# Building self-attention's fused weights from 32-column matmuls in four column groups, each matrix as its load lands, and issuing later stages' weights in other periods

## The reference, cut to what matters

```python
q_lat = (x @ Wq_down).reshape(b, t, H, L)      # 16 heads, latent size 64
k_lat = (x @ Wk_down).reshape(b, t, H, L)
v_lat = (x @ Wv_down).reshape(b, t, H, L)
q_c = jnp.einsum('bthl,ld->bhtd', q_lat, Wq_up_c)   # and q_e, k_c, k_e
v = jnp.einsum('bthl,ld->bhtd', v_lat, Wv_up)
q = jnp.concatenate([q_c, _apply_rope(q_e, cos, sin)], axis=-1)
...
att = jax.nn.softmax(scores, axis=-1)
return y @ Wc
...
x = _layernorm(x + _L0_attn_ref(x, ...), axis=-1)
```

## Time and profile before

| | |
|---|---|
| median of three runs | 2525.32 us (2520.55 to 2530.87) |
| profiled execution | 2539.31 us |
| its span | 2537.5 us |
| its mean granted TensorE clock | 0.887 |
| self-attention's share | about the first 397 us |

### The profile page before, as it was taken

The page is one execution under the profiler, slowest core; times in us unless marked ns, Lnnn a source line. Parts: engine busy times, 40 slices in busy tenths (PEclk is TensorE's granted clock), DMA queues, the critical chain, the costliest instruction groups (busy, mean ns, idle before and its releaser), DMA issues. The chain is left out here.

```text
span 2537.5 us, 58466 instructions
## 1 busy us (share of the span) xinstructions
PE 2118.6 (83%) x20310; PEld 1583.7 (62%) x20310; DVE 1530.8 (60%) x3550; ACT 950.6 (37%) x1881; POOL 928.1 (37%) x913
## 2 busy tenths in 40 slices
PE   6999997999776664788489996999999999996575
PEld 4666665777676554566388884666666666664233
DVE  1444443555454546233255455799999999984898
ACT  1444442333210110233134342344444444442897
POOL 0111111111134555223355431455555555553343
PEclk9999998999887786899789897899999999997555
DMA  6000003555311110877233311011110101000111
GB/s 208 30 29 29 29 25 130 207 205 212 133 48 35 34 33 23 259 222 221 73 100 90 98 44 46 21 32 31 32 32 23 32 31 32 30 13 9 52 58 46
DMA packets 157643, 192.74 MB, mean 76 GB/s; under 512 B 28517, under 2 KB 141160, under 8 KB 157559
## 3 DMA queue, kind: packets, MB, share of 16 engines
q1 hardware_dynamic: 147287, 189.03, 23.7%
q0 software_dynamic: 10272, 2.62, 0.5%
HBM read 140.74 MB, written 77.51 MB: 86 GB/s over the span
## 5 line engine op out<-in xcount | busy, mean ns | idle before, releaser
L2757 ACT ACTIVATE xa_prob<-xa_A 121x1600 f32<-121x1600 f32 x96 | 144.5, 1505 | 304.1 <-PE xa_A L2636 304.1
L2828 POOL TENSOR_TENSOR xa_prob<-xa_prob,xa_exp_bias 121x1600 f32<-121x1600 f32 x64 | 228.7, 3573 | 41.0 <-ACT xa_prob L2757 40.9
L2929 DVE TENSOR_REDUCE xa_kq<-xa_A 100x4 f32<-100x1444 f32 x128 | 211.6, 1653 | 21.3 <-PE xa_A L2609 21.1
L1409 POOL DMA_INDIRECT slot_rows<-rt_x_again,rt_slot_u x150 | 152.6, 1017 | 166.0 <-DVE rt_x_again L1527 103.5
L2909 DVE TENSOR_SCALAR xa_rows_n<-xa_rows_t,xa_mv,xa_rstd 121x256 f32<-121x256 f32 x128 | 142.4, 1172 | 1.1 <-POOL xa_rstd L2845 1.1
L2636 PEld LDWEIGHTS xa_A<-xa_q2T,xa_kqT 17*121 17x121 f32 x3072 | 93.9, 185 | 56.5 <-DVE xa_kq L2929 35.9
L696 DVE TENSOR_REDUCE sa_kq<-sa_A 100x16 f32<-100x1600 f32 x32 | 58.4, 1826 | 106.1 <-PE sa_A L457 106.1
L2609 PE MATMUL xa_A<-xa_kqT 16*100 16x361 f32 x1024 | 112.9, 510 | 9.9 <-ACT xa_prob L2757 6.8
L2636 PE MATMUL xa_A<-xa_q2T,xa_kqT 17*121 17x100 f32 x3072 | 109.3, 280 | 13.8 <-DVE xa_kq L2929 13.2
L1655 POOL DMA_INDIRECT contrib<-ex_y,ex_place_u x64 | 62.3, 973 | 158.5 <-ACT ex_y L1707 140.4
L2850 POOL TENSOR_TENSOR xa_o_rstd<-xa_o_var,xa_power 100x1 f32<-100x1 f32 x32 | 17.9, 560 | 252.1 <-DVE xa_o_var L2969 252.1
(11 more groups left out here) (350 smaller groups left out, 5397.0 us busy)
## 6 DMA issues: line engine op xcount, KB each, us to landing
ex_w<-in_w13T SPq DMA_DIRECT2D x64, 352.0 KB
contrib<-xs_zero SPq DMA_DIRECT2D x30, 640.0 KB
la_rows<-contrib SPq DMA_DIRECT2D x16, 1200.0 KB
xs_ctxT<-in_ctxT SPq DMA_DIRECT2D x32, 512.0 KB
xa_rows_t<-in_ctx SPq DMA_DIRECT2D x96, 121.0 KB
ex_w<-in_w2T SPq DMA_DIRECT2D x64, 176.0 KB
slot_rows<-xs_zero SPq DMA_DIRECT2D x32, 272.0 KB
ex_x_t<-slot_rows SPq DMA_DIRECT2D x64, 136.0 KB, 2.2
```

Source lines behind the costliest of these rows:

```text
L1409: nc.gpsimd.indirect_dma_start(slot_rows, bass.IndirectOffsetOnAxis(slot_u[:, k, n:n + 1], 0), x_again[:, k, :], None, bounds_check=SLOTS ...
L2757: nc.scalar.activation(prob[:, n, :].rearrange("p (h a) -> p h a", h=HPG), A[:ROWS, :, 0:G * T], ACT.Exp, scale=EXP_SCALE).then_inc(exp_re ...
L2828: nc.gpsimd.tensor_tensor(chunk, chunk, exp_bias[:, n, :].unsqueeze(1).to_broadcast([ROWS, HEADS, T]), ALU.mult).then_inc(biased, 1)
L2929: nc.vector.tensor_reduce(kq[:T, k, NCH, 4 * j:4 * j + 4, DH:DH + 1].rearrange("p h o -> p (h o)"), A[:T, :, 0:src_len], axis=AXIS_X, op=A ...
```

## The change

`up` is put together on the host as one array `L0_attn_up` (128x3x2x16, zeros included) and loaded by one DMA; its memset and the waits for it go. The loads have semaphores of their own (`up_in` for up and ident, `down_in[k]` for each `down`), SyncE's order is up, down 0, ident, the first rows, down 1, down 2, wc, cos, sin, causalf, and it no longer waits for them.

TensorE's matmuls change sides: the 32 columns of `up` are stationary, 256 columns of `down` move, and the result (32x256, the fused weights turned on their side) goes to one of four groups of 32 PSUM partitions: 24 matmuls instead of 48. ScalarE copies each matrix (128x512) to `turned_w`; TensorE turns it back with four 128x128 transposes into `C[k]`; VectorE copies it to `wqk` or `wv`. TensorE's order is fuse(0), fuse(1), turn(0), fuse(2), turn(1), turn(2). VectorE's casts of ident and causalf stand behind its three copies; ScalarE waits for all three copies before its loop.

SyncE issues the later stages' weights in periods -1 to 3, now behind `residual` and ahead of `store`: strided in -1, cross in 0, ffn in 1, route and lists in 2, linear in 3.

```diff
--- before.py
+++ after.py
@@ -281,6 +281,7 @@
         s = Store(nc, ctx, "sa", 2)
         down = s.sb("down", [P, 3, HEADS // 2, D])
         up = s.sb("up", [P, 3, 2, DH])
+        turned_w = s.sb("turned_w", [P, 3, 2 * D])
         wqk = s.sb("wqk", [P, KC, 2 * D])
         wv = s.sb("wv", [P, KC, D])
         wc = s.sb("wc", [P, KC, D])
@@ -316,8 +317,9 @@
         C = [s.ps(f"C{k}", [P, 512]) for k in range(4)]
 
         w_in = s.sem("weights_loaded")
-        up_zero, up_ready, cleared = s.sem("up_zero"), s.sem("up_ready"), s.sem("cleared")
+        up_in, down_in, cleared = s.sem("up_in"), [s.sem(f"down_in{k}") for k in range(3)], s.sem("cleared")
         fused, fused_sb = s.sem("fused_in_psum"), s.sem("fused_in_sbuf")
+        fused_turned, turned_w_ready = s.sem("fused_turned"), s.sem("turned_w_ready")
         const_ready, power_set = s.sem("const_ready"), s.sem("power_set")
         x_loaded = [s.sem(f"x_loaded{k}") for k in range(2)]
         res_loaded = [s.sem(f"res_loaded{k}") for k in range(2)]
@@ -334,7 +336,7 @@
         yT_turned, yT_ready, o_done, r_ready = (s.sem(n) for n in ("yT_turned", "yT_ready", "o_done", "r_ready"))
         o_stats_ready, o_mv_ready, o_var_ready, o_rstd_ready = (s.sem(n) for n in ("o_stats_ready", "o_mv_ready", "o_var_ready", "o_rstd_ready"))
         out_ready = s.sem("out_ready")
-        W_ALL = 16 * 18
+        W_ALL = 16 * 4
         FIRST, LAST, REACH, LOW = -3, 3, 4, 4
 
         with nc.Block() as block:
@@ -359,30 +361,25 @@
                     sp.wait_ge(out_ready, at(b, 1, 1))
                     sp.dma_start(x_out[b[0] * 2 + b[1]], x_o[:, k, :]).then_inc(stored[k], 16)
 
+                sp.dma_start(up[:], w["L0_attn_up"]).then_inc(up_in, 16)
                 for k, name in enumerate(("L0_attn_Wq_down", "L0_attn_Wk_down", "L0_attn_Wv_down")):
-                    sp.dma_start(down[:, k, :, :], w[name].rearrange("(h l) c -> l h c", l=P)).then_inc(w_in, 16)
-                sp.wait_ge(up_zero, 1)
-                for head, part in ((0, slice(0, 64)), (1, slice(64, 128))):
-                    for k, (c_, e_) in enumerate((("Wq_up_c", "Wq_up_e"), ("Wk_up_c", "Wk_up_e"))):
-                        sp.dma_start(up[part, k, head, 0:E2], w["L0_attn_" + c_]).then_inc(w_in, 16)
-                        sp.dma_start(up[part, k, head, E2:DH], w["L0_attn_" + e_]).then_inc(w_in, 16)
-                    sp.dma_start(up[part, 2, head, :], w["L0_attn_Wv_up"]).then_inc(w_in, 16)
-                sp.dma_start(ident[:], w["ident"]).then_inc(w_in, 16)
+                    sp.dma_start(down[:, k, :, :], w[name].rearrange("(h l) c -> l h c", l=P)).then_inc(down_in[k], 16)
+                    if k == 0:
+                        sp.dma_start(ident[:], w["ident"]).then_inc(up_in, 16)
+                        rows((0, 0))
                 sp.dma_start(wc[:], w["L0_attn_Wc"].rearrange("(k p) n -> p k n", p=P)).then_inc(w_in, 16)
                 sp.dma_start(cos[:], w["cos_sa_rows"]).then_inc(w_in, 16)
                 sp.dma_start(sin[:], w["sin_sa_rows"]).then_inc(w_in, 16)
                 sp.dma_start(causalf[:], w["causal"]).then_inc(w_in, 16)
-                rows((0, 0))
-                sp.wait_ge(w_in, W_ALL)
 
                 def body(b, has):
                     if has(4):
                         rows(later(b, 4))
-                    if b[1] < 0:
-                        for held in later_weights[b[1] - FIRST::-FIRST]:
-                            held.load(sp)
                     if has(-1):
                         residual(later(b, -1))
+                    if -1 <= b[1] < LOW:
+                        for held in later_weights[b[1] + 1]:
+                            held.load(sp)
                     if has(-3):
                         store(later(b, -3))
 
@@ -395,15 +392,32 @@
                 for sem, per in ((x_turned, 1), (qk_done, 1), (kq_turned, 2), (scored, 1), (q2_turned, 1), (shifted, 1), (v_done, 1),
                                  (av_done, 1), (y_turned, 1), (yT_turned, 1), (o_done, 1)):
                     pe.sem_inc(sem, per * LEAD)
+                pe.wait_ge(up_in, 32)
+
+                def fuse(k):
+                    pe.wait_ge(down_in[k], 16)
+                    for h in range(HEADS // 2):
+                        m, g = divmod(h, 4)
+                        last = nc.tensor.matmul(A[32 * g:32 * g + 32, k, m * D:(m + 1) * D], up[:, k, :, :].rearrange("p two d -> p (two d)"),
+                                                down[:, k, h, :], start=True, stop=True)
+                    last.then_inc(fused, 1)
+
+                def turn_fused(k):
+                    pe.wait_ge(turned_w_ready, k + 1)
+                    for c in range(KC):
+                        for m in range(KC):
+                            o = c * D + m * P
+                            last = nc.tensor.transpose(C[k][:, o:o + P], turned_w[:, k, m * D + c * P:m * D + (c + 1) * P], ident[:])
+                    last.then_inc(fused_turned, 1)
+
+                fuse(0)
+                fuse(1)
+                turn_fused(0)
+                fuse(2)
+                turn_fused(1)
+                turn_fused(2)
                 pe.wait_ge(w_in, W_ALL)
-                pe.wait_ge(up_zero, 1)
-                for k in range(3):
-                    for c in range(KC):
-                        for h in range(HEADS // 2):
-                            last = nc.tensor.matmul(A[:, k, c * D + 2 * h * DH:c * D + 2 * (h + 1) * DH], down[:, k, h, c * P:(c + 1) * P],
-                                                    up[:, k, :, :], start=True, stop=True)
-                last.then_inc(fused, 1)
-                pe.wait_ge(fused_sb, 1)
+                pe.wait_ge(fused_sb, 3)
                 pe.wait_ge(const_ready, 1)
 
                 def turn_rows(b):
@@ -557,11 +571,11 @@
                 for sem, per in ((xT_ready, 1), (copied, 1), (kqT_ready, 2), (q2_ready, 1), (exp_ready, 1), (v_ready, 1), (oT_ready, 1),
                                  (yT_ready, 1)):
                     act.sem_inc(sem, per * LEAD)
-                act.wait_ge(fused, 1)
-                for k, dst in ((0, wqk[:, :, D:2 * D]), (1, wqk[:, :, 0:D]), (2, wv[:])):
-                    last = nc.scalar.activation(dst, A[:, k, :].rearrange("p (c n) -> p c n", n=D), ACT.Copy)
-                last.then_inc(fused_sb, 1)
+                for k in range(3):
+                    act.wait_ge(fused, k + 1)
+                    nc.scalar.activation(turned_w[:, k, :], A[:, k, :], ACT.Copy).then_inc(turned_w_ready, 1)
                 act.wait_ge(cleared, 2)
+                act.wait_ge(fused_sb, 3)
 
                 def queries_out(b):
                     act.wait_ge(q2_turned, at(b, 1, 1))
@@ -669,7 +683,6 @@
 
             @block.vector
             def _(dve):
-                nc.vector.memset(up[:], 0.0).then_inc(up_zero, 1)
                 nc.vector.memset(v1[:], 1.0)
                 nc.vector.memset(kq[:], 0.0).then_inc(cleared, 1)
                 dve.wait_ge(cleared, 1)
@@ -677,6 +690,15 @@
                 for sem, per in ((roped, 1), (max_ready, 1), (rec_ready, 1), (y_ready, 1), (r_ready, 1), (o_stats_ready, 1), (o_mv_ready, 1),
                                  (o_var_ready, 1), (out_ready, 1)):
                     dve.sem_inc(sem, per * LEAD)
+
+                def fused_out(k, dst):
+                    dve.wait_ge(fused_turned, k + 1)
+                    nc.vector.tensor_copy(dst, C[k][:].rearrange("p (c n) -> p c n", n=D)).then_inc(fused_sb, 1)
+
+                fused_out(0, wqk[:, :, D:2 * D])
+                fused_out(1, wqk[:, :, 0:D])
+                fused_out(2, wv[:])
+                dve.wait_ge(up_in, 32)
                 dve.wait_ge(w_in, W_ALL)
                 nc.vector.tensor_copy(identb[:], ident[:T, :T])
                 nc.vector.tensor_copy(causal[:], causalf[:]).then_inc(const_ready, 1)
@@ -3455,7 +3477,7 @@
     lists_w = ExpertLists(nc, w)
     route_w = RouteWeights(nc, w)
     strided_w = StridedWeights(nc, w)
-    self_attention(nc, NB, x, x1, w, (strided_w, route_w, lists_w, linear_w, cross_w, ffn_w))
+    self_attention(nc, NB, x, x1, w, ((strided_w,), (cross_w,), (ffn_w,), (route_w, lists_w), (linear_w,)))
     cross_attention_strided(nc, NB, x1, x2, w, src_len, slot_rows, contrib, strided_w)
     route(nc, NB, x2, w, slot_rows, xz, route_w, ffn_w)
     experts(nc, NB, w, slot_rows, contrib, lists_w)
@@ -3531,8 +3553,12 @@
     o = {}
     for k in ("Wq_down", "Wk_down", "Wv_down"):
         o["L0_attn_" + k] = x["L0_attn_" + k].T
-    for k in ("Wq_up_c", "Wq_up_e", "Wk_up_c", "Wk_up_e", "Wv_up", "Wc"):
-        o["L0_attn_" + k] = x["L0_attn_" + k]
+    ups = [np.concatenate([x["L0_attn_" + n] for n in names], 1) for names in (("Wq_up_c", "Wq_up_e"), ("Wk_up_c", "Wk_up_e"), ("Wv_up",))]
+    o["L0_attn_up"] = np.zeros((P, 3, 2, DH), ups[0].dtype)
+    for k, up in enumerate(ups):
+        for head in range(2):
```

(2 more changed lines are left out.)

## The result

In the first comparison the changed kernel takes 2517.64 us, the median of eight runs (2505.72 to 2526.04); before takes 2531.51 us over its eight (2520.55 to 2539.12). The ratio is 0.9944, with a 95% interval of 0.9916 to 0.9971: faster by 14 us, between 7 and 21. The forecast was 2504 us, within 2492 to 2515, from a saving of 21 us. The direction held, and so did the saving in the place where it was forecast; the time lies 2.6 us above the range. Two later comparisons of the same kernel gave 0.9894 (0.9866 to 0.9922) and 0.9904 (0.9868 to 0.9940), 27 and 24 us. Three executions with a mean granted clock of 0.34 to 0.73 (3076.70 us of before; 2756.41 and 6005.97 us of the old fused part with the new periods) enter no ratio.

The account below looks back on a forecast made before the run. The serial prologue before the loop was taken as exposed: its chain 12.7 + 2.2 + 1.0 + 1.0 + 0.7 + 0.34 + 0.2 = 18.1 us instead of 39.27 saves 21.2, so 2525.3 - 21.2 = 2504.1 us, range 2492 to 2515.

Parts of the forecast that it names:

- third `down` there: Prologue loads: last byte of the third `down` at 12.5 us, 0.2 to its semaphore, so 12.7, at most 14.5.
- hops: Prologue chain: 0.2 us in all for handing over between engines.
- all terms are for the slow clock: Prologue: TensorE taken at half rate, 1.2 GHz, for every term of the chain, until about 66 us in before.
- rival 1: Loop start: clock already up before the loop, so its 11 us slow start goes too: 2493 us; chance 0.13.
- the long fused stretch ahead of the loop changes nothing about the clock: Prologue: 20.7 us of busy matmuls hadn't raised the clock, so the loop's start was expected slow for about the same stretch.
- a rise one period earlier or later: Loop start: the clock rising a period sooner or later moves the end by some 5 us, most of the range.
- Column groups that don't overlap: Prologue matmuls: groups run one after another, 7.5 us a matrix instead of 2.2, giving 2519 us; chance 0.09.
- Bundles in the way: Self-attention periods: later-weight bundles in SyncE's queue delay `rows` or stores; 2531 us if all 26.6 us are exposed; chance 0.03.
- Saved time given back: Loop start: a slow stretch two periods (10 us) longer, or SyncE stalling on the third `down`: 2514 us; chance 0.1.
- the base of the sum: Whole kernel: the median of before, 2525.3 us, from which the 21.2 us saving was subtracted.
- theory B: Stages behind self-attention: the change makes them give back some 8 us; 2146 to 2150 us there, 10 to 16 faster overall.
- theory A: Stages behind self-attention: they spread from run to run whatever stands ahead; the prologue's 21 us are all kept.

Follow-up runs that it names:

- old fused part with the new periods: Kernel before, fused part unchanged, with the later weights issued in the new periods -1 to 3: ratio to before 1.0006 (0.9972 to 1.0040).
- filler: Changed kernel plus matmuls with unused results where TensorE waits, in the prologue and periods -3 to -1: 2497.74 us over 6 runs, ratio to before 0.9883.
- old matmuls: Changed kernel's loads and waits for each matrix, with the old matmuls (32 moving columns, no turn): 2526.45 us in one run, before 2510.68.
- eight in one group: Changed kernel with eight more matmuls behind matrix 0's, all in column group 0: 2369.23 us in one run, before 2387.10.
- after, second: The changed kernel again, no edit: 2505.42 us over 12 runs, ratio to before 0.9894 (0.9866 to 0.9922).
- after, third: The changed kernel a third time, no edit, beside the second filler run: ratio to before 0.9904 (0.9868 to 0.9940).
- old periods: Changed kernel with the later weights issued in periods -3 to -1, ahead of the residuals, as before: 2502.20 us over 6 runs, ratio to before 0.9892.
- filler, second: The kernel with filler matmuls in prologue and periods -3 to -1 again, beside the changed kernel: ratio to before 0.9874 (0.9846 to 0.9902).
- pairs: Changed kernel with a matrix's matmuls in order 0, 4, 1, 5, 2, 6, 3, 7, so neighbours share a column group: 2502.38 us in one run, before 2510.68.
- all in: Changed kernel, but TensorE waits for all weights before fuse(0): 2519.80 us in one run, before 2510.68.
- late filler: Changed kernel with filler matmuls only behind turn_fused(2) and in periods -3 to -1: 2379.89 us in one run, before 2387.10.

## Why the prediction was right or wrong

**The chain, term by term.**

| term | forecast | measured |
|---|---|---|
| third `down` there | 12.7 (at most 14.5) | 13.85 |
| fuse(2) | 2.2 | 1.75 |
| turn(1), turn(2) | 2.0 | 1.45 |
| VectorE copy of 512 columns | 0.7 | 0.69 |
| casts | 0.34 | 0.32 |
| hops | 0.2 | 0.26 |
| first `turn_rows` | 18.1 | 18.2 |

The end is right to 0.1 us by luck, for two errors cancel. The load came 1.2 us later than I took, inside the bound. In its first 13.8 us the profile has 263 GB/s, 3.6 MB, which is 0.3 MB more than the loads up to the third `down` hold. Either bytes of the loads behind it were moved among its own, or its semaphore came some 0.8 us behind its last byte; the traces don't tell which. The matmuls were faster, because my "all terms are for the slow clock" was wrong behind 15 us: eight turns took 1.45 us where four had taken 1.12. That is the beginning of rival 1. (Fuse, turn, fuse, turn changes the mode three times, not four as I wrote; no term hangs on it.)

**The clock in the loop's start.** The granted clock of the changed kernel (stretch, us, busy time of each engine, granted clock, DMA) shows a middle course between my forecast and rival 1:

```profile
17.00:18.00 1.00, 0.00 (x0) 0.00 (x0) 0.93 (x3) 0.00 (x0) 0.00 (x0) 1.00 0.00 0
18.00:19.00 1.00, 0.36 (x2) 0.20 (x2) 0.00 (x0) 0.23 (x1) 0.00 (x0) 0.85 0.00 0
19.00:20.00 1.00, 0.84 (x1) 0.41 (x2) 0.00 (x0) 0.11 (x1) 0.00 (x0) 0.50 0.21 63
22.00:23.00 1.00, 0.57 (x2) 0.00 (x0) 0.39 (x2) 0.00 (x0) 0.00 (x0) 0.94 0.00 0
25.00:26.00 1.00, 0.56 (x7) 0.36 (x5) 0.00 (x0) 0.75 (x2) 0.00 (x0) 0.76 0.53 159
26.00:27.00 1.00, 0.80 (x3) 0.55 (x4) 0.00 (x0) 0.15 (x1) 0.00 (x0) 0.50 0.88 303
32.00:33.00 1.00, 0.76 (x2) 0.00 (x0) 0.20 (x1) 0.00 (x0) 0.00 (x0) 0.82 0.07 23
33.00:34.00 1.00, 0.00 (x0) 0.00 (x0) 0.56 (x2) 0.38 (x1) 0.37 (x1) 1.00 0.00 0
```

It falls at 18.7, around the first `turn_rows`, is back from 22.1 to 25.5, falls again and is up from 32.4 on; so it had risen before 18.7. In before, by the durations, it came up near 66 us, 27 us into the loop. The fills with filler, 36.8 and 36.9 us, are what the same steps take at full rate. By them the slow clock in the fill costs 46.5 - 36.8 = 9.7 us in before (forecast 11) and 4.4 in the changed kernel. That accounts for the 25 us in self-attention in this pair of profiles: 21.1 from the chain and 5.3 from an earlier rise, of which 1 to 2 are lost in its other periods. I had said that the long fused stretch ahead of the loop changes nothing about the clock. That held for the old matmuls, also in the new loads (`keys_and_queries` still takes 3.73 us at 41.29 there), and not for the new ones.

The 5.3 us are one pair. The other profile with the old fused part has a fill of 42.7 us and `keys_and_queries` at 1.96 us a period earlier than before has it; against it the changed kernel's fill is only 1.5 us shorter. This part of the forecast, a rise one period earlier or later that moves the end by some 5 us, came true. By the start of `cross_attention_strided` (404.3 and 406.7 us with the old fused part, 380.6 to 382.7 in the five profiles with the new one, neither filler nor a longer wait) the change saves 22 to 26 us. At the end the three comparisons give 14, 27 and 24 us. Weighted by their intervals they come to 21 us, give or take 4, so whether the gain at the end is 21 or 25 isn't shown.

The Trainium skill, TensorE: Matmul & The Clock Gate, "What's actually happening", has the clock follow recent activity; the traces agree: matmuls in the gaps kept it at full rate through the fill in three of three profiles, and without them it fell again in all seven profiles in which it had risen ahead of the loop. The Trainium skill, TensorEngine Tiling, "Key Properties", has a change of mode drain TensorE; the traces show no cost of it: turn(0) ends at 13.83 and fuse(2) starts at 13.85, in the moment in which its load is there too.

**Rivals.** The clock up before the loop: in part, as told. Column groups that don't overlap: refuted by the eight in one group. Bundles in the way: no wait, and two comparisons with nothing. Saved time given back: 9 us were missing at the end of the first trace, but not by the mechanism that I named, and not because of the change.

**The step that failed: the base of the sum, and the spread of the untouched stages, which I put at nothing.** I wrote that the profiled execution of before stood 14 us above the median and that no term depends on why, took the median of three runs as the base, and named the clock in the loop's start, some 5 us, as most of my range. Eleven profiles, on chips on which these stages took alike, show what that left out. Behind self-attention the stages took, from `cross_attention_strided`'s start to the end of the span:

| kernel | us | `linear_attention` | its granted clock | `cross_attention` |
|---|---|---|---|---|
| before | 2130.8 | 296.4 | 0.89 | 794.8 |
| after | 2139.7 | 300.0 | 0.88 | 794.8 |
| after, second | 2139.7 | 300.7 | 0.87 | 794.1 |
| after, third | 2129.4 | 287.6 | 0.91 | 790.2 |
| old periods | 2121.4 | 293.9 | 0.89 | 790.4 |
| old fused part, new periods | 2125.9 | 290.0 | 0.91 | 794.8 |
| filler | 2113.0 | 286.3 | 0.92 | 790.4 |
| filler, second | 2140.0 | 299.1 | 0.88 | 794.4 |
| pairs | 2119.2 | 289.8 | 0.91 | 794.6 |
| all in | 2133.1 | 302.1 | 0.87 | 794.7 |
| old matmuls | 2128.4 | 299.0 | 0.88 | 789.8 |

The sum ranges over 27 us, and one kernel covers it alone: 2113.0 and 2140.0 with filler. The changed kernel has 2129.4 beside 2139.7, so theory B's mark of 2148 (counted from self-attention's last instruction) isn't its own: its third profile has 2137.9 there. The nine profiles with the new loads average 2129.3 us, the two with the old ones 2128.4. Most of the spread is TensorE's clock. Two kernels' rows for `linear_attention`, first the filler's, then that with all weights awaited (columns: stretch, us, busy of PE, PEld, DVE, ACT, POOL, granted clock, DMA share, GB/s):

```profile
1230.00:1516.30 286.30, 257.09 (x1821) 230.11 (x1821) 151.61 (x454) 114.47 (x269) 139.13 (x122) 0.92 0.29 82
```

```profile
1236.70:1538.80 302.10, 273.35 (x1820) 244.76 (x1821) 150.67 (x454) 115.00 (x269) 137.91 (x122) 0.87 0.27 77
```

`linear_attention` works through the same instructions in 286.3 us at 0.92 and in 302.1 at 0.87. The busy time of TensorE's matmuls grows by 16.3 us with it, and that of VectorE, ScalarE and GpSimd stays within 1.3 us. The two executions of one kernel that lie 27 us apart, those with filler, say the same. Their sums over `route`, `experts`, `linear_attention` and `cross_attention` are:

```profile
sum 1638.30, PE 1361.38 PEld 1043.04 DVE 1066.38 ACT 546.64 POOL 764.97; mean PE 340.34 PEld 260.76 DVE 266.60 ACT 136.66 POOL 191.24
sum 1665.70, PE 1387.77 PEld 1063.60 DVE 1067.13 ACT 548.58 POOL 764.07; mean PE 346.94 PEld 265.90 DVE 266.78 ACT 137.15 POOL 191.02
```

The second took 27.4 us longer, with TensorE's matmuls busy for 26.4 us more and VectorE, ScalarE and GpSimd for the same time within 2 us. Over the eleven profiles, with the granted clock as it is printed, to two decimals, `linear_attention`'s time grows by 0.48 us for each us spent at half rate (correlation 0.99), `experts`' by 0.45 (0.95), `route`'s by 0.51 (0.86). `cross_attention` has only two printed values, 789.8 to 790.4 us at 0.96 in four profiles and 794.1 to 794.8 at 0.95 in seven. The clock falls and rises again within these stages, and how much of a stage is spent at half rate differs from run to run.

So theory A holds: the 9 us were not given back by the change. The terms that were mis-sized are the base and the range. The base, the median of three runs, 2525.3, was 6 us too low for the eight runs of the first comparison (2531.5), and 9 and 14 for those of the two later ones (2534.3 and 2539.1). With 2531.5 my own saving gives 2510.3, inside the range that I had stated. The other 7 us are the first comparison's saving of 14 instead of 21. They lie within what the untouched stages spread: half of their 27 us on either side of 2504 alone give 2490.5 to 2517.5, and the measured 2517.6 is at the edge of that.

What stays open: which of the stages' gaps makes the clock fall in one run and not in the next. The traces show the fall, not its cause to the microsecond. Why the first comparison shows 14 us and the two others 27 and 24 is open too: chance, the chip or the time. The intervals of the first and the second touch only at 0.992. Whether the filler's 3 to 5 us reach the end in full was not resolved by 12 runs of it.

## What to carry to other kernels

A prologue that nothing overlaps is worth its whole length, and each term of its chain can be forecast to about a microsecond from rows of the same shape at the same clock. Start each matrix when its load lands, give small matrices the stationary side, and spread them over column groups; the two orders tried here took the same time. A saving of 1% needs more than a sum, though: before stating a range, ask how much the untouched stages spread, and take their granted clock in the profile as the first suspect. If the profiled execution stands 14 us off the median, the range has to be at least that wide until the cause is known, and three runs are too few for a base.

## What the runs showed of the hardware

**A second matmul for the same column group doesn't hold back the next group.** With neighbours in the same group a matrix took 1.96 us, with neighbours in different groups 1.93. The profile has the starts of four records together and the next four 0.43 us later in both.

**The profile's granted clock reads 1.00 until its first change.** In before it reads 1.00 at 39 to 66 us, where `keys_and_queries` took 3.73 us and later 1.96. Durations of one line at two places tell the level there.

**One chip ran two stages much faster.** The kernels with one group and with the late filler were run on another chip than the rest, where before took 2387.10 us in its one run (2510.68 beside the pairs). Their spans are 2367.4 and 2378.1 us, with the same prologue and the same `cross_attention_strided` (290.6 and 290.5), but `route` took 232.8 and 234.4 us where the eleven others have 324.7 to 333.3, and `experts` 196.1 and 195.1 where they have 231.2 to 244.2. `route`'s rows, first on the other chips (the changed kernel's third profile), then on this one:

```profile
671.50:1004.20 332.70, 209.53 (x1269) 189.36 (x1269) 168.26 (x590) 35.34 (x108) 151.96 (x150) 0.75 0.14 39
```

```profile
671.40:904.20 232.80, 184.31 (x1268) 167.81 (x1268) 168.20 (x590) 34.90 (x108) 154.25 (x150) 0.87 0.21 55
```

VectorE, ScalarE and GpSimd (POOL) are busy for the same time in both within 2.3 us, and TensorE for 25 us more at its lower clock, so most of the 100 us are waiting. What is waited for can't be read from the names in these traces. In the first, 26 waits of up to 10.9 and 13.8 us carry the name of a load of self-attention, but the instructions wait for semaphores that only TensorE raises in this stage. What makes the stage slower there is open. For this case it means that times are compared within one comparison only, on one chip.
